# A four-layer graph network on one core: the last expert sums over edges before its own rows, and the closing scale and clip move

## The chip, the cores and the metric

The kernel runs on one core of one Trainium2 chip. The metric is the device time of one execution in microseconds (us), the median of several runs.

## The reference, cut to what matters

512 nodes with 512 features each pass through four graph layers; each layer sees `h = max(layernorm(x), 0)` and its result is added to `x`. The change lies in the end of the third layer and in the fourth.

```python
# layer 3: four experts of two convolutions each, the two best per node
def sage_conv(h, W_l, b_l, W_r):
    aggr = segment_sum(h[src], dst) * inv_deg
    return aggr @ W_l + b_l + h @ W_r
for e in range(4):
    h = x
    for l in range(2):
        h = relu(sage_conv(h, Wl[e, l], bl[e, l], Wr[e, l]))
out = sum over the top 2 experts of gate * h
# layer 4: graph convolution with self loops
H = X @ W + b
out = relu(segment_sum(H[src_f] * coef[:, None], dst_f))   # coef = isd[src] * isd[dst]
# and around each layer
h = max(layernorm(x), 0);  x = x + layer(h)
```

## The kernel before

Nodes are four row tiles of 128 (`NT = 4`), features four column tiles (`DT = 4`). The edges are held as a 512 x 512 matrix of counts, so each sum over edges is a matrix product. A float32 product is made of rounded parts: a matrix is split into `hi` and `lo`, and `mm3` (L1146 to L1148) multiplies hi by hi, hi by lo and lo by hi. The counts are exact, so a sum over edges (`sums_over_edges`, L1174 and L1175) takes two products for a tile, and a plain float32 product takes one instruction that the chip runs as two passes.

The order of all work is written out by hand, one instruction stream for each engine, with semaphores between them. PSUM (`ps`) has eight banks of 128 x 512 float32.

For each expert `e` TensorE makes, in this order: the hidden rows in banks 0 to 3; `z = hidden @ Wl` in banks 4 to 7; the expert's own rows `hidden @ Wr` in banks 0 to 3 (48 products); and the sum over edges of `z` in banks 4 to 7 (32 products). `z` is split by ScalarE (`z_hi`, L675) and VectorE (`z_lo`, L1069). VectorE adds the bias row `row_bl` to own rows (L1076, into `part`), ScalarE scales `part` by the node's gate (L682), VectorE adds the edge sums scaled by `inv_gate` (L1105), and clips and adds this to `x_sb` (L1110). `inv_gate` and `beats` are one buffer; it is made at L1078.

Behind the last expert comes the layer norm `LN5`. For each tile VectorE takes the statistics (L713 to L715), GpSimd a power (`rstd`, L471), VectorE the shift (L723), and ScalarE writes the normalised tile `h_sb` (L533). The last summation multiplies `h_sb` by `loop_hi`, the counts with self loops. The first `WHOLE` tiles go in as plain float32 (L1522), the others in two parts: `R_hi` by ScalarE (L690), `R_lo` by VectorE (L1118), products L1525 and L1526. The sum is split again (`agg_hi` L693, `agg_lo` L1122) and multiplied by the last weights; VectorE adds the bias row `b3_row` scaled by `reach` (L1135), ScalarE scales by `isd` and clips (L696), VectorE adds the mark of nodes without edges, `no_edge_nan`, and `x_sb` (L1130), and SyncE sends each tile out (L431). GpSimd makes the `lo` part of each weight matrix (L452, L453) and ScalarE the `hi` part (L528).

The order of the last expert's summation on TensorE is set by this piece:

```python
pe.wait_ge(z_lo_made, NT * (e + 1))
sums_over_edges(4, c_hi, c_lo, z_hi, z_lo, z_lo_made, NT * e, 1, near_done)
```

`together` (here 1) is the number of k tiles that are multiplied for all four goals before the rest is done goal by goal. Of VectorE's closing loops:

```python
norm_shift(LN5, NT - 1)
for t in range(WHOLE, NT):
    v.wait_ge(last_hi_made, t - WHOLE + 1)
    # R_lo[t] = h_sb[t] - R_hi[t]
```

Of the kernel before, what the change touches and what calls it, by code (L numbers as in the profile page):

```python
# [39 lines left out]
def build(nc, d, out):  # L40
# [193 lines left out]
    WHOLE = 2  # L234
# [10 lines left out]
    with ctx:  # L245
# [80 lines left out]
        last_done, last_sum, last_relu, x4_made = sem("last_done"), sem("last_sum"), sem("last_relu"), sem("x4_made")  # L326
# [197 lines left out]
        def _(act):  # L524
# [140 lines left out]
            for e in range(EXPERTS):  # L665
# [18 lines left out]
                if e < EXPERTS - 1:  # L684
                    split_hi(u + 5)
# [8 lines left out]
            for t in range(NT):  # L694
                act.wait_ge(last_sum, t + 1)
                nc.scalar.activation(tmp[:, t, :], tmp[:, t, :], ACT.Relu, scale=isd[:, t:t + 1])\  # L696
                  .then_inc(last_relu, 1)


        @block.vector  # L700
        def _(v):
# [291 lines left out]
            link(nc.vector.tensor_tensor(reach[:], reach[:], isd[:], ALU.add))  # L993

# [60 lines left out]

            for e in range(EXPERTS):
# [14 lines left out]
                v.wait_ge(bl_in[e % 2], 16 * (e // 2 + 1))  # L1071
# [29 lines left out]

                for t in range(NT):
                    v.wait_ge(near_done, NT * e + t + 1)
                    v.wait_ge(own_gated, NT * e + t + 1)
                    nc.vector.scalar_tensor_tensor(part[:, t, :], ps[:, 4 + t, :], inv_gate[:, t:t + 1],  # L1105
                                                   part[:, t, :], ALU.mult, ALU.add).then_inc(expert_sum, 1)
# [19 lines left out]
            b3_row = wait_row(B3)  # L1126

            def finish(t):
                v.wait_ge(last_relu, t + 1)
                nc.vector.scalar_tensor_tensor(x_sb[:, t, :], tmp[:, t, :], no_edge_nan[:, t:t + 1], x_sb[:, t, :],  # L1130
                                               ALU.add, ALU.add).then_inc(x4_made, 1)

            for t in range(NT):
                v.wait_ge(last_done, t + 1)
                nc.vector.scalar_tensor_tensor(tmp[:, t, :], b3_row[:], reach[:, t:t + 1], ps[:, 4 + t, :],  # L1135
                                               ALU.mult, ALU.add).then_inc(last_sum, 1)
                if t >= 1:
                    finish(t - 1)
            finish(NT - 1)


        @block.tensor
        def _(pe):
# [324 lines left out]
            for e in range(EXPERTS):  # L1468
# [25 lines left out]
                hi, lo = weights(FIRST_EXPERT + 4 * e + 3)  # L1494
                for t in range(NT):
                    for k in range(DT):
                        last = mm3(ps[:, t, :], hid_hi[:, k, col(t)], hid_lo[:, k, col(t)], hi[:, k, :],
                                   lo[:, k, :], k == 0, k == DT - 1)
                    last.then_inc(own_done, 1)

                pe.wait_ge(z_lo_made, NT * (e + 1))
                sums_over_edges(4, c_hi, c_lo, z_hi, z_lo, z_lo_made, NT * e, 1, near_done)


            pe.wait_ge(own_made, NT * EXPERTS)
# [62 lines left out]
```

## Time and profile before

| | us |
|---|---|
| median of 3 runs | 498.01 |
| the runs | 497.74, 500.13, 498.01 |
| the profiled execution's own time | 497.47 |
| its span | 495.7 |
| TensorE busy in the span | 458.0 (92%) |
| VectorE, ScalarE, GpSimd busy | 306.9, 192.0, 164.2 |

The span is what the profiler saw of one execution; the device time is 1.77 us longer. In the rows PE is TensorE, DVE VectorE, ACT ScalarE, POOL GpSimd, SP SyncE. Matmuls overlap in the array, so the distance between two starts says what one costs, not its length. The mean granted clock of TensorE over the span is 0.978 of full.

### The profile page before, as it was taken

The numbers are of one execution on the slowest core, as the hardware profiler recorded it, in microseconds if no ns is written. First come the engines' busy times: TensorE is split into PE (matmuls) and PEld (weight loads), VectorE is DVE, ScalarE is ACT, GpSimd is POOL, SyncE is SP. The second block draws the span as 40 slices with busy tenths as digits, with TensorE's granted clock in tenths as the row PEclk, the third lists the DMA queues.
The fourth block names the chain that finished last, engine by engine and source line by source line (L and its number), as shares of the span: only waits on it lengthen the run. The fifth ranks groups of instructions, "written<-read, shape, count | busy, mean of one in ns | idle before, by whom it ended". The sixth has DMA issues, their size and how long they took to land.

```text
span 495.7 us, 5939 instructions
## 1 busy us (share of the span) xinstructions
PE 458.0 (92%) x2107; PEld 334.1 (67%) x2107; DVE 306.9 (62%) x574; ACT 192.0 (39%) x264; POOL 164.2 (33%) x107
## 2 busy tenths in 40 slices
PE   4999996889869899899899999999999999999996
PEld 2465442334346778678678888888888888888654
DVE  5999836999975994877685333622362237133654
ACT  5888516546130631142441335123422252224232
POOL 3000131112243984448150433443344334343000
PEclk9999999899979999889998999999999999999999
DMA  8750000000030224203220032203420242120002
GB/s 265 202 225 1 1 1 22 0 1 0 1 106 0 72 100 170 85 1 117 77 86 0 19 127 110 86 2 109 161 87 3 91 141 89 41 85 1 0 1 85
DMA packets 22474, 34.34 MB, mean 69 GB/s; under 512 B 5680, under 2 KB 5936, under 8 KB 22448
## 3 DMA queue, kind: packets, MB, share of 16 engines
q1 hardware_dynamic: 22160, 33.85, 20.2%
q8 instruction: 18, 0.29, 0.2%
q10 hardware_dynamic: 288, 0.13, 0.1%
q14 instruction: 8, 0.07, 0.0%
HBM read 32.93 MB, written 1.05 MB: 69 GB/s over the span
## 4 chain that ended last, share of the span: by engine, by line
PE 63%; DVE 20%; issue 6%; POOL 5%; ACT 3%; DVEq 3%; DMA 1%; POOLq 0%
PE ps L1146 16%; PE ps L1148 16%; PE ps L1147 16%; PE ps L1208 4%; DVE one_src L784 3%; PE ps L1174 3%; PE ps L1175 3%; DVE rsum L886 2%; DVEq L784 2%; DVE e_sb L373 2%; DVE stats L713 2%; POOL x_sb L477 1%; PE ps L1287 1%; POOL w_lo L453 1%; PE ps L1159 1%
## 5 line engine op out<-in xcount | busy, mean ns | idle before, releaser
L452 POOL TENSOR_TENSOR w_lo<-w_stage,w_hi 128x1024 fp32r<-128x1024 f32 x22 | 52.7, 2395 | 137.7 <-ACT w_hi L528 137.7
L528 ACT ACTIVATE w_hi<-w_stage 128x2048 fp32r<-128x2048 f32 x23 | 43.9, 1910 | 73.1 <-PE ps L1148 73.1
L453 POOL TENSOR_TENSOR w_lo<-w_stage,w_hi 128x1024 fp32r<-128x1024 f32 x22 | 57.4, 2607 | 0.0
L1146 PE MATMUL ps<-w_hi,hid_hi 128*128 128x512 f32 x128 | 49.8, 389 | 0.0
L1147 PE MATMUL ps<-w_lo,hid_hi 128*128 128x512 f32 x128 | 49.8, 389 | 0.0
L1148 PE MATMUL ps<-w_hi,hid_lo 128*128 128x512 f32 x128 | 49.8, 389 | 0.0
L1063 DVE TENSOR_SCALAR tmp<-ps,bl 128x512 f32<-128x512 f32 x16 | 12.0, 751 | 52.2 <-ACT hid_hi L670 52.2
L1146 PE MATMUL ps<-T_hi,w_hi 128*128 128x512 f32 (+1 forms) x112 | 41.6, 372 | 1.8 <-DVE T_lo L743 1.4
L1148 PE MATMUL ps<-T_hi,w_lo 128*128 128x512 f32 (+1 forms) x112 | 40.7, 363 | 0.0
L1147 PE MATMUL ps<-T_lo,w_hi 128*128 128x512 f32 (+1 forms) x112 | 40.7, 363 | 0.0
L471 POOL TENSOR_TENSOR rstd<-vareps,scalars 128x1 f32<-128x1 f32 x24 | 15.8, 660 | 59.4 <-DVE vareps L715 59.4
L784 DVE TENSOR_SCALAR one_src<-iota_n,edge_m,edge_w 128x256 f16 x128 | 34.0, 332 | 0.0
L477 POOL TENSOR_TENSOR h_sb<-h_sb,row 128x512 f32<-128x512 f32 x8 | 11.1, 1403 | 55.8 <-DVE digits L798 48.7
L1076 DVE TENSOR_TENSOR part<-ps,row_bl 128x512 f32<-128x512 f32 x16 | 11.1, 691 | 29.9 <-PE ps L1148 29.9
L1069 DVE TENSOR_TENSOR z_lo<-ps,z_hi 128x512 fp32r<-128x512 f32 x16 | 10.9, 691 | 29.1 <-ACT z_hi L675 29.1
L1159 PE MATMUL ps<-ident,h_sb 128*128 128x128 f32 x64 | 13.5, 354 | 16.0 <-ACT h_sb L533 11.1
L608 ACT ACTIVATE s_bf<-ps 128x1024 bf16<-128x1024 f32 x16 | 16.4, 1023 | 30.4 <-PE ps L1287 22.3
L1147 PEld LDWEIGHTS ps<-w_lo,hid_hi 128*128 128x128 f32 x128 | 24.0, 188 | 5.0
L1146 PEld LDWEIGHTS ps<-w_hi,hid_hi 128*128 128x128 f32 x128 | 24.0, 188 | 5.0
L1148 PEld LDWEIGHTS ps<-w_hi,hid_lo 128*128 128x128 f32 x128 | 24.0, 188 | 5.0
L491 POOL TENSOR_TENSOR pool_sum<-e_sb 128x512 f32<-128x512 f32 x7 | 8.9, 1267 | 51.2 <-DVE rsum L884 31.6
L1146 PEld LDWEIGHTS ps<-T_hi,w_hi 128*128 128x128 f32 x112 | 21.6, 193 | 5.6 <-DVE T_lo L743 1.7
(206 smaller groups left out, 1064.4 us busy)
## 6 DMA issues: line engine op xcount, KB each, us to landing
w_stage<-in_L_gnn_Wr SPq DMA_DIRECT2D x8, 1024.0 KB, 5.3
w_stage<-in_L_gnn_Wl SPq DMA_DIRECT2D x8, 1024.0 KB, 5.2
w_stage<-in_L_gnn_W SPq DMA_DIRECT2D x5, 1024.0 KB, 6.3
x_sb<-in_x SPq DMA_DIRECT2D x4, 256.0 KB, 3.6
w_q<-in_L_gnn_Wq SPq DMA_DIRECT2D x1, 1024.0 KB, 7.8
w_k<-in_L_gnn_Wk SPq DMA_DIRECT2D x1, 1024.0 KB, 10.1
w_v<-in_L_gnn_Wv SPq DMA_DIRECT2D x1, 1024.0 KB, 5.7
w_o<-in_L_gnn_Wo SPq DMA_DIRECT2D x1, 1024.0 KB, 9.6
```

The lines of the kernel that those rows point to most:

```text
L452: gp.tensor_tensor(w_lo[s][:, 0:2], stage[s][:, 0:2], f32(w_hi[s][:, 0:2]), ALU.subtract)
L453: gp.tensor_tensor(w_lo[s][:, 2:4], stage[s][:, 2:4], f32(w_hi[s][:, 2:4]), ALU.subtract)\
L471: gp.tensor_tensor(rstd[:, n - 1:n], vareps[:, n - 1:n], half_neg, ALU.pow).then_inc(ln_rstd, 1)
L477: ins = gp.tensor_tensor(target[:, t, :], target[:, t, :], row[slot][:], ALU.add)
L528: nc.scalar.activation(w_hi[u % 2][:], stage[u % 2][:], ACT.Copy).then_inc(hi_made, 1)
L608: nc.scalar.activation(heads.rearrange("p (w b) n -> p w b n", w=2), group_scores(i, g), ACT.Copy)\
L784: last = nc.vector.tensor_scalar(one_src[:, bass.ds(slot, 1), :].squeeze(1), iota_n[:, 0:HALF], edge_m[:, 0, bass.ds(c, 1)], edge_w[:, bas ...
L1146: nc.tensor.matmul(goal, a_hi, b_hi, start=start, stop=False, **kw)
L1147: nc.tensor.matmul(goal, a_hi, b_lo, start=False, stop=False, **kw)
L1148: return nc.tensor.matmul(goal, a_lo, b_hi, start=False, stop=stop, **kw)
L1159: last = nc.tensor.transpose(ps[:, bank, col(j)], h_sb[:, t, col(j)], ident[:])
L1208: last = nc.tensor.matmul(ps[:, bank, :], src[:, k, col(t)], w[:, k, :], start=k == 0, stop=k == DT - 1)
```

## The change

1. In the last expert (`e == EXPERTS - 1`) TensorE sums over edges first, into banks 0 to 3 and with `together` 3, and makes own rows behind it, into banks 4 to 7.
2. ScalarE no longer scales own rows there; it writes `part = row_bl * gate` beforehand. VectorE adds the edge sums (`near_part`), then own rows scaled by the gate (`last_own`), which takes the place of L1105 in front of L1110. The additions of L1076 go for this expert.
3. `WHOLE` is 1: one plain tile in the last summation, three in two parts.
4. ScalarE writes the last bias row, scaled by `reach * isd`, into `tmp` before `LN5`; VectorE multiplies `reach` by `isd` once, in layer 2. VectorE adds `no_edge_nan` to `x_sb` beforehand (four instructions). At the end one VectorE instruction scales by `isd` and adds the bias, a second clips and adds to `x_sb`; ScalarE's clip L696 is gone.

```diff
-    WHOLE = 2
+    WHOLE = 1
...
@@ scalar
+                if e == EXPERTS - 1:
+                    act.wait_ge(bl_in[e % 2], 16 * (e // 2 + 1))
+                    for t in range(NT):
+                        act.wait_ge(x3_made, NT * e)
+                        nc.scalar.activation(part[:, t, :], row_bl[e % 2][:], ACT.Copy, scale=gate[:, t, e:e + 1])                          .then_inc(bl_gated, 1)
+                    break
...
+            act.wait_ge(reach_made, 1)
...
+            for t in range(NT):
+                nc.scalar.activation(tmp[:, t, :], row[b3_slot][:], ACT.Copy, scale=reach[:, t:t + 1])                  .then_inc(bias_row_made, 1)
...
-            for t in range(NT):
-                act.wait_ge(last_sum, t + 1)
-                nc.scalar.activation(tmp[:, t, :], tmp[:, t, :], ACT.Relu, scale=isd[:, t:t + 1])\
-                  .then_inc(last_relu, 1)
@@ vector
+            nc.vector.tensor_tensor(reach[:], reach[:], isd[:], ALU.mult).then_inc(reach_made, 1)
...
+            def near_part(e, t):
+
+                v.wait_ge(bl_gated, t + 1)
+                v.wait_ge(near_done, NT * e + t + 1)
+                nc.vector.scalar_tensor_tensor(part[:, t, :], ps[:, t, :], inv_gate[:, t:t + 1], part[:, t, :],
+                                               ALU.mult, ALU.add).then_inc(near_added, 1)
+
+            def last_own(e, t):
+
+                v.wait_ge(own_done, NT * e + t + 1)
+                v.wait_ge(near_added, t + 1)
+                nc.vector.scalar_tensor_tensor(part[:, t, :], ps[:, 4 + t, :], gate[:, t, e:e + 1], part[:, t, :],
+                                               ALU.mult, ALU.add).then_inc(expert_sum, 1)
...
-                for t in range(NT):
+                if e < EXPERTS - 1:
+                    v.wait_ge(bl_in[e % 2], 16 * (e // 2 + 1))
+                for t in range(NT if e < EXPERTS - 1 else 0):
...
+                if e == EXPERTS - 1:
+                    for t in range(NT):
+                        near_part(e, t)
...
-            b3_row = wait_row(B3)
+            for t in range(NT):
+                v.wait_ge(ln_out, ln_out_no(LN5, t))
+                nc.vector.tensor_scalar(x_sb[:, t, :], x_sb[:, t, :], no_edge_nan[:, t:t + 1], None, ALU.add)                  .then_inc(nan_added, 1)
 
             def finish(t):
-                v.wait_ge(last_relu, t + 1)
-                nc.vector.scalar_tensor_tensor(x_sb[:, t, :], tmp[:, t, :], no_edge_nan[:, t:t + 1], x_sb[:, t, :],
-                                               ALU.add, ALU.add).then_inc(x4_made, 1)
+                v.wait_ge(last_sum, t + 1)
+                v.wait_ge(nan_added, t + 1)
+                nc.vector.scalar_tensor_tensor(x_sb[:, t, :], tmp[:, t, :], 0.0, x_sb[:, t, :], ALU.max, ALU.add)                  .then_inc(x4_made, 1)
 
             for t in range(NT):
                 v.wait_ge(last_done, t + 1)
-                nc.vector.scalar_tensor_tensor(tmp[:, t, :], b3_row[:], reach[:, t:t + 1], ps[:, 4 + t, :],
+                v.wait_ge(bias_row_made, t + 1)
+                nc.vector.scalar_tensor_tensor(tmp[:, t, :], ps[:, 4 + t, :], isd[:, t:t + 1], tmp[:, t, :],
                                                ALU.mult, ALU.add).then_inc(last_sum, 1)
-                if t >= 1:
-                    finish(t - 1)
-            finish(NT - 1)
+                finish(t)
@@ tensor
+                if e < EXPERTS - 1:
+                    own_rows(0)
+                    pe.wait_ge(z_lo_made, NT * (e + 1))
+                    sums_over_edges(4, c_hi, c_lo, z_hi, z_lo, z_lo_made, NT * e, 1, near_done)
+                else:
+
+                    sums_over_edges(0, c_hi, c_lo, z_hi, z_lo, z_lo_made, NT * e, NT - 1, near_done)
+                    own_rows(4)
...
-            pe.wait_ge(own_made, NT * EXPERTS)
+            pe.wait_ge(near_added, NT)
```

TensorE's instructions where the last expert ends and the last summation begins, before. L1174 and L1175 are edge sums, L1522 the plain tiles, L1525 and L1526 the tiles in two parts; in brackets is what an instruction waits for.

```order
L1174 MATMUL ps<-z_hi,c_hi 128x512
L1175 MATMUL ps<-z_lo,c_hi 128x512
L1522 MATMUL ps<-loop_hi,h_sb 128x512 [waits ln_out,loop_made,own_made]
L1522 MATMUL ps<-loop_hi,h_sb 128x512 x3
L1522 MATMUL ps<-loop_hi,h_sb 128x512 [waits ln_out]
L1522 MATMUL ps<-loop_hi,h_sb 128x512 x3
L1525 MATMUL ps<-loop_hi,R_hi 128x512 [waits last_lo_made]
L1526 MATMUL ps<-loop_hi,R_lo 128x512
```

The same place in the changed kernel, where L1178 and L1179 are own rows, L1560 the plain tile, L1563 and L1564 the tiles in two parts:

```order
L1178 MATMUL ps<-w_lo_54,hid_hi 128x512
L1179 MATMUL ps<-w_hi_52,hid_lo 128x512
L1560 MATMUL ps<-loop_hi,h_sb 128x512 [waits ln_out,loop_made,near_added]
L1560 MATMUL ps<-loop_hi,h_sb 128x512 x3
L1563 MATMUL ps<-loop_hi,R_hi 128x512 [waits last_lo_made]
L1564 MATMUL ps<-loop_hi,R_lo 128x512
```

Own rows now stand directly ahead of the last summation, and the second tile waits for `R_lo` where it waited for `h_sb`.

VectorE's instructions from the last shift on, before:

```order
L723 SCALAR_TENSOR_TENSOR shift<-moments,rstd 128x1 [waits ln_rstd]
L1118 TENSOR_TENSOR R_lo<-h_sb,R_hi 128x512 [waits last_hi_made] x2
L1122 TENSOR_TENSOR agg_lo<-ps,agg_hi 128x512 [waits mix_hi_made] x4
L1135 SCALAR_TENSOR_TENSOR tmp<-row_110,node_cols,ps 128x512 [waits last_done,row_in0]
L1135 SCALAR_TENSOR_TENSOR tmp<-row_110,node_cols,ps 128x512 [waits last_done]
L1130 SCALAR_TENSOR_TENSOR x_sb<-tmp,node_cols,x_sb 128x512 [waits last_relu]
```

and in the changed kernel (`node_cols` holds `isd`, `reach` and `no_edge_nan`):

```order
L731 SCALAR_TENSOR_TENSOR shift<-moments,rstd 128x1 [waits ln_rstd]
L1148 TENSOR_TENSOR R_lo<-h_sb,R_hi 128x512 [waits last_hi_made] x3
L1152 TENSOR_TENSOR agg_lo<-ps,agg_hi 128x512 [waits mix_hi_made] x4
L1158 TENSOR_SCALAR x_sb<-x_sb,node_cols 128x512 [waits ln_out] x4
L1168 SCALAR_TENSOR_TENSOR tmp<-ps,node_cols,tmp 128x512 [waits bias_row_made,last_done]
L1163 SCALAR_TENSOR_TENSOR x_sb<-tmp,x_sb 128x512 [waits nan_added,last_sum]
```

There is a third `R_lo` behind the last shift, four additions stand between `agg_lo` and the closing pair, and the second of that pair waits for VectorE's own first.

## Rows read from the trace of the kernel before

**Rows 1.** The chain of waits, from the last expert's end: start us, us, what

```profile
461.01 2.47 issue
...
490.92 0.76 DVE tmp L1135
491.69 0.73 ACT tmp L696
492.45 0.75 DVE x_sb L1130
```

**Rows 2.** Timeline of PE: start us, us, engine line op out<-in, count, idle before

```profile
449.16 0.39 PE L1146 MATMUL ps<-w_hi,hid_hi 128*128 128x512 f32 x1
...
459.81 0.39 PE L1148 MATMUL ps<-w_hi,hid_lo 128*128 128x512 f32 x1
...
467.07 0.39 PE L1175 MATMUL ps<-z_lo,c_hi 128*128 128x512 f32 x1
467.97 7.11 PE L1522 MATMUL ps<-loop_hi,h_sb 128*128 128x512 f32 x16 [0.51 <-ACT h_sb L533]
475.49 0.50 PE L1525 MATMUL ps<-loop_hi,R_hi 128*128 128x512 f32 x1 [0.41 <-DVE R_lo L1118]
...
477.50 0.50 PE L1525 MATMUL ps<-loop_hi,R_hi 128*128 128x512 f32 x1
...
479.73 0.47 PE L1146 MATMUL ps<-w_hi,agg_hi 128*128 128x512 f32 x1
```

**Rows 3.** Timeline of DVE over the same stretch

```profile
447.95 2.73 DVE L1069 TENSOR_TENSOR z_lo<-ps,z_hi 128x512 fp32r<-128x512 f32 x4 [7.27 <-ACT z_hi L675]
...
460.24 0.69 DVE L1076 TENSOR_TENSOR part<-ps,row_bl 128x512 f32<-128x512 f32 x1 [2.03 <-PE ps L1148]
...
463.48 0.75 DVE L1105 SCALAR_TENSOR_TENSOR part<-ps,beats,part 128x512 f32<-128x512 f32 x1 [2.48 <-issue]
464.27 0.69 DVE L1110 SCALAR_TENSOR_TENSOR x_sb<-part,x_sb 128x512 f32<-128x512 f32 x1
...
466.07 0.74 DVE L1105 SCALAR_TENSOR_TENSOR part<-ps,beats,part 128x512 f32<-128x512 f32 x1
...
471.31 0.74 DVE L1105 SCALAR_TENSOR_TENSOR part<-ps,beats,part 128x512 f32<-128x512 f32 x1
...
474.67 0.16 DVE L723 SCALAR_TENSOR_TENSOR shift<-moments,rstd 128x1 f32<-128x1 f32 x1 [0.66 <-POOL rstd L471]
474.75 0.68 DVE L1118 TENSOR_TENSOR R_lo<-h_sb,R_hi 128x512 fp32r<-128x512 f32 x1
...
478.90 2.48 DVE L1122 TENSOR_TENSOR agg_lo<-ps,agg_hi 128x512 fp32r<-128x512 f32 x4 [1.83 <-ACT agg_hi L693]
```

**Rows 4.** L1105 over the whole span: ns min/median/max, first and last start

```profile
L1105 DVE SCALAR_TENSOR_TENSOR part<-ps,beats,part x16: 739/741/752, 311.1 to 471.3; 128x512 f32<-128x512 f32 x16
```

**Rows 5.** Timeline of ACT

```profile
449.85 1.91 ACT L528 ACTIVATE w_hi<-w_stage 128x2048 fp32r<-128x2048 f32 x1
...
460.97 0.72 ACT L682 ACTIVATE part<-part,gate 128x512 f32<-128x512 f32 x1 [2.00 <-DVE part L1076]
...
475.71 0.63 ACT L690 ACTIVATE R_hi<-h_sb 128x512 fp32r<-128x512 f32 x1
```

**Rows 6.** Timeline of POOL where the first L1105 ran

```profile
311.25 2.40 POOL L452 TENSOR_TENSOR w_lo<-w_stage,w_hi 128x1024 fp32r<-128x1024 f32 x1 [6.96 <-ACT w_hi L528]
```

**Rows 7.** The page, costliest groups: a VectorE operation with a scalar operand on 256 columns

```profile
L784 DVE TENSOR_SCALAR one_src<-iota_n,edge_m,edge_w 128x256 f16 x128 | 34.0, 332 | 0.0
```

**Rows 8.** Timeline of DVE in layer 2, where `reach` is made

```profile
231.08 2.32 DVE L993 TENSOR_TENSOR node_cols<-node_cols 128x4 f32<-128x4 f32 x1
...
236.72 0.69 DVE L998 TENSOR_TENSOR x_sb<-ps,x_sb 128x512 f32<-128x512 f32 x1 [1.40 <-PE ps L1148]
```

**Rows 9.** Two stretches: us, busy us (instructions) of each engine, granted clock, DMA

```profile
208.00:210.00 2.00, 1.09 (x4) 0.72 (x4) 1.89 (x6) 0.73 (x3) 0.55 (x1) 0.50 0.00 0
...
467.30:475.49 8.19, 7.27 (x18) 2.97 (x17) 7.14 (x18) 3.41 (x5) 1.65 (x3) 1.00 0.00 0
```

**Rows 10.** The chain of waits at the low clock, in layer 2

```profile
212.34 0.43 PE ps L1147
```

More of the change, by code:

```diff
@@ L325, in build @@
         mix_done, mix_hi_made, mix_lo_made = sem("mix_done"), sem("mix_hi_made"), sem("mix_lo_made")
-        last_done, last_sum, last_relu, x4_made = sem("last_done"), sem("last_sum"), sem("last_relu"), sem("x4_made")
+        last_done, last_sum, x4_made = sem("last_done"), sem("last_sum"), sem("x4_made")
+        bias_row_made, nan_added, reach_made = sem("bias_row_made"), sem("nan_added"), sem("reach_made")
+        bl_gated, near_added = sem("bl_gated"), sem("near_added")
         stored = sem("stored")
@@ L683, in _ @@
                       .then_inc(own_gated, 1)
-                if e < EXPERTS - 1:
-                    split_hi(u + 5)
+                split_hi(u + 5)
+            act.wait_ge(reach_made, 1)
+            b3_slot = rows_in[B3][1]
+            act.wait_ge(row_in[b3_slot], 16 * (1 + sum(s == b3_slot for _, s in rows_in[:B3])))
+            for t in range(NT):
+                nc.scalar.activation(tmp[:, t, :], row[b3_slot][:], ACT.Copy, scale=reach[:, t:t + 1])                  .then_inc(bias_row_made, 1)
             for t in range(NT):
@@ L1100, in _ @@
                         v.wait_ge(loop_lo_made, 3 * NT + 1)
+                if e == EXPERTS - 1:
+                    for t in range(NT):
+                        near_part(e, t)
                 for t in range(NT):
[L1103 to L1106, printed above, removed]
+                    if e == EXPERTS - 1:
+                        last_own(e, t)
+                    else:
+                        v.wait_ge(near_done, NT * e + t + 1)
+                        v.wait_ge(own_gated, NT * e + t + 1)
+                        nc.vector.scalar_tensor_tensor(part[:, t, :], ps[:, 4 + t, :], inv_gate[:, t:t + 1],
+                                                       part[:, t, :], ALU.mult, ALU.add).then_inc(expert_sum, 1)
                     if e == EXPERTS - 1 and t >= 1:
@@ L1493, in _, with own_rows @@
                             last.then_inc(z_done, 1)
[L1494 to L1502, printed above, removed]
-            pe.wait_ge(own_made, NT * EXPERTS)
+                def own_rows(bank):
+                    hi, lo = weights(FIRST_EXPERT + 4 * e + 3)
+                    for t in range(NT):
+                        for k in range(DT):
+                            last = mm3(ps[:, bank + t, :], hid_hi[:, k, col(t)], hid_lo[:, k, col(t)], hi[:, k, :],
+                                       lo[:, k, :], k == 0, k == DT - 1)
+                        last.then_inc(own_done, 1)
+                if e < EXPERTS - 1:
+                    own_rows(0)
+                    pe.wait_ge(z_lo_made, NT * (e + 1))
+                    sums_over_edges(4, c_hi, c_lo, z_hi, z_lo, z_lo_made, NT * e, 1, near_done)
+                else:
+                    sums_over_edges(0, c_hi, c_lo, z_hi, z_lo, z_lo_made, NT * e, NT - 1, near_done)
+                    own_rows(4)
+            pe.wait_ge(near_added, NT)
             pe.wait_ge(loop_made, NT)
```

1 line of the change is left out of this document (removed).

## The prediction, made before the changed kernel was run

> **What bounds the kernel now.** I read the chain of waits first. Up to 461.01 it is TensorE without a break, then a stretch that no engine holds alone, and the end is VectorE, ScalarE, VectorE on one tile [rows 1]. Then the timelines of TensorE and VectorE side by side from 449 us on. The reader should see three things in them.
>
> First, up to 467.07 TensorE issues a product each 0.227 us: 48 of own rows from 449.16 to 460.04 (10.88 us), 32 of edge sums behind them, 7.26 us [rows 2]. Then VectorE takes over. Its work for a tile (L1105, L1110, the statistics) repeats each 2.6 us, 463.48 to 466.07 [rows 3], but edge sums come out goal by goal, the first at about 463 and the last at 467.5, so three tiles queue up on VectorE. The fourth L1105 starts at 471.31, 3.8 us after TensorE had finished its bank. Second, from that start to the first product in two parts there are 4.18 us: 471.31 to 475.49, through `rstd`, the shift at 474.67 and `R_lo` at 474.75, which stands behind it [rows 2, 3]. Third, TensorE has little to do in that time: two plain tiles in 16 passes, 7.11 us, so about 0.43 from one to the next [rows 2]. The end of the program hangs on the fourth tile's layer norm, not on TensorE.
>
> **Edge sums first.** The swap leaves 80 products where there were 80, so TensorE is through at the same time if it never waits. The edge sums need `z_lo`; the first tile is ready at about 447.95 + 0.68 = 448.6, half a microsecond ahead of 449.16, and the fourth at 450.68, while k = 3 is first asked for after 24 products, at 454.6 [rows 3]. So no wait, and `together` 3 is what makes the third k tile wait for nothing. Own rows come out each 2.72 us (12 products), the last with the product at 467.07. VectorE started on an own row 0.43 us after its last product (459.81 to 460.24) [rows 2, 3], so the four `last_own` start at about 459.34, 462.06, 464.78 and 467.50. VectorE needs 2.6 us for a tile and gets one each 2.72: it keeps up, with 0.1 us to spare. The fourth starts at 467.50 in place of 471.31: **3.81 us** earlier on VectorE's side. `last_own` has L1105's form, 0.74 us [rows 4].
>
> What must be ready: the four `part = row_bl * gate` stand on ScalarE behind the weight copy that ends at 451.76, at most 0.72 each [rows 5], so they end by 454.6; the first edge sum needs 24 + 2 products, the last of them issued at 449.16 + 25 x 0.227 = 454.84, and VectorE sees it 0.43 us later, at about 455.3. Four `near_part` of at most 0.75 end by 458.3, one microsecond ahead of the first `last_own`. They run while GpSimd splits weights. So did the first L1105, at 311.1 with GpSimd's L452 from 311.25 on [rows 4, 6], and all 16 of them took 739 to 752 ns: none was held up. The four L1076 at 0.69 go; they were idle time's.
>
> **One plain tile.** Two plain tiles from 467.6 on would hold TensorE for 16 x 0.43 = 6.9 us, to about 474.5. One holds it to about 471.1. The second tile now needs `R_lo`, which stands behind the last shift: by the 4.18 us above it starts at 467.50 + 4.18 = 471.68. TensorE idles some 0.6 us there, then does three tiles. A tile took 475.49 to 477.50, 2.01 us with the start and the branch in it [rows 2]; a following one I put at 8 x 0.233 = 1.87. So the fourth tile starts at 471.68 + 2.01 + 1.87 = 475.56, against 477.50. `R_hi` of the fourth tile (before 475.71 to 476.34 [rows 5]) ends 3.8 us earlier, at 472.5, and its `R_lo` at 473.3: no wait. **Gain at the fourth tile 1.94 us.** From there to 479.73 and on to the last L1135 at 490.92 the work is the same, moved as a whole. So of the 3.81 us, 1.87 go to the third tile in two parts; with two plain tiles TensorE would be the bound and the gain about 0.9 us less.
>
> **The closing pair.** Before, L1135, ScalarE's L696 and L1130 start at 490.92, 491.69 and 492.45 and end at 493.20, 2.28 us [rows 1]. Now two instructions of VectorE follow each other as L1105 and L1110 do: 463.48 to 464.27 is 0.79, and the second has L1110's form, 0.69 [rows 3]; 1.48 us. **Gain 0.80 us.** By the cycle table of the Trainium skill (VectorE: DVE Perf Modes, the section on the TRN2 errata, 58 cycles plus one for each element from SBUF to SBUF) an estimate of the second instruction is 0.59 us and the gain would be 0.1 us larger; the row has 0.69, and I go by the row.
>
> **The rest, at nothing.** The four additions of `no_edge_nan` have no counterpart in the trace. Bounds: 0.33 us (scalar form on half as many columns [rows 7]) and 0.75 (an operation that reads PSUM too [rows 4]); I take 0.69, that of a full SBUF tile. They start when `agg_lo` ends, 481.38 - 1.94 = 479.44 [rows 3], and end by 482.4 at the upper bound; the first tile's closing pair begins three tiles of 2.04 us (9 products) before the fourth's, at 490.92 - 1.94 - 6.12 = 482.9. After that the pair's 1.48 us fit between tiles. The four scaled bias rows of ScalarE run from 454.6 to 457.5, the first normalisation starts at about 463. The product `reach * isd` in layer 2 follows an instruction that took 2.32 us on four columns; 1.40 us later VectorE idles for TensorE [rows 8]. I take 0.15 us, at most 2.3, of which 1.4 are covered: 0, at most 0.9. Output copies: one each 2.04 us, the last as long as before.
>
> **The sum** is 1.94 + 0.80 = 2.74 us. The profiled execution (497.47, span 495.7) becomes 494.7 (span 493.0). It lies 0.54 below the median of the runs shown; from that median, 498.01 - 2.74 = **495.3 us**, 0.55% less. About 0.5%, 2.5 us, is what a measurement of this kernel can tell from no change, so the forecast is just past it.
>
> **Rivals.**
>
> *VectorE falls behind by tiles.* The margin is 0.1 us for each of three tiles. If a tile costs 2.9 us in place of 2.6 (two semaphores to wait for where it was one), the fourth `last_own` starts at 459.34 + 3 x 2.9 = 468.04, 0.5 us late; if `near_part` also ends 1 us behind its cover, 1.5 us late. The time is 495.8 to 496.8, no change by the bound. For it: the margin is small. Against it: four tiles before ran at 2.6 in each case. Chance 0.22, with the reach product's 0.9 us in it.
>
> *More than forecast.* The span ends 2.5 us behind the last L1130 (493.20 to 495.7), and the third tile's copy was issued only 0.9 us ahead of the fourth's; now they are 2.04 us apart. If 0.4 us of the 2.5 were that, and the later tiles of the summation start 0.2 us quicker than I put them, the time is 494.7. Chance 0.1.
>
> *The change of order is hidden*: TensorE waits at 449.16 for `z_lo` and everything behind moves by what the sum gains. That takes `z_lo` late by 3 us where the trace has it 0.5 us early. Time 498. Chance 0.04.
>
> *Slower: the clock.* At 208 to 210 TensorE was busy 1.09 of 2 us and its granted clock stood at 0.50, the lower of its two levels, 1.2 GHz [rows 9]; products then came each 0.43 us [rows 10], not 0.227. The change puts a new idle piece at 471.1 to 471.7, ahead of 24 + 48 = 72 products on the path. At the low level each costs 0.2 us more: all of them 14.6 us, a time of 509.9. It decides from 26 of the 72 on (2.74 + 2.5 us over 0.2). Against it: in the stretch of 8.19 us that has both idle pieces of before, 0.51 and 0.41, the clock was 1.00 throughout [rows 2, 9], and the new order has half the plain passes and one idle piece, with own rows issued densely ahead of it. The Trainium skill (TensorE: Matmul & The Clock Gate, on the clock gate) says that the throttled state is the default and that only activity lifts it; by that rule a thinner stretch here is what could bring it down. Chance 0.04.
>
> *The change does not do what it says.* The orders above show it on both engines; what could fail is only that the waits bind elsewhere, which is the first rival.
>
> **How the numbers follow.** Forecast 0.6, VectorE behind 0.22, more 0.1, hidden 0.04, clock 0.04. The predicted time is the forecast's, 495.3. The range: down to 494.3, which is the 494.7 of the case with more and 0.4 us for the spread of the runs (two of the three are 0.27 apart); up to 496.8, the end of the first rival; the two unlikely ones are left out. Faster by over 0.5% means below 495.5: most of the forecast's 0.6 (0.53 of it, as it passes the bound by only 0.25 us), and the 0.1 of the case with more: 0.63. Within 0.5%: the rest of the forecast, the first rival and the hidden case, 0.33. Slower: the clock, 0.04.
>
> **What would show it.** In the profile after: edge sums of the last expert from 449.2 without a gap; the fourth `last_own` near 467.5; one plain tile of eight passes; the first product in two parts near 471.7 and the fourth tile's near 475.6; the four `no_edge_nan` additions over before the first closing pair; closing pair of 1.5 us with no ScalarE in it; clock 1.00 to the end. It is wrong if VectorE's `last_own` starts later than 0.5 us after its own row's last product, if `R_lo` of the fourth tile is what its products wait for, or if the closing instructions queue.

## The result, and the profile after the change

The changed kernel takes **494.5 us** (median of 7 runs, 493.78 to 496.18), the kernel before 498.01 (497.56 to 500.13 in the 7 runs beside it). The ratio is 0.9923, with a 95% interval of 0.9903 to 0.9943: 0.8% less, where 0.55% was forecast. By the ratio that is 3.8 us, a time of 494.2; by the medians it is 3.5; the forecast was 2.74. The sign was right, the gain larger.

The profiled execution took 493.78 us (span 491.9, before 495.7). The summary of the profile's page hides nearly all of the change: TensorE has the same 2107 products and the same share of the span.

```profile
span 491.9 us, 5957 instructions
...
PE 454.6 (92%) x2107; PEld 333.7 (68%) x2107; DVE 309.4 (63%) x580; ACT 192.4 (39%) x265; POOL 164.3 (33%) x107
```

So I went to the end of the chain of waits, as before [rows 1] (start us, us, what):

```profile
467.30 2.13 issue
...
470.20 0.61 DVE R_lo L1148
470.86 0.50 PE ps L1563
...
475.31 0.61 ACT agg_hi L706
475.95 0.70 DVE agg_lo L1152
476.79 0.47 PE ps L1177
...
487.97 0.76 DVE tmp L1168
488.75 0.69 DVE x_sb L1163
```

No ScalarE stands in the closing part any more. The chain passes from the layer norm to TensorE at 470.86, which is the second tile, and from there on TensorE does not wait until `agg_hi`. Before, the chain's last release came later, at the third tile. The timeline of TensorE shows the places that the forecast named (start us, us, engine line op out<-in, count, idle before and what ended it):

```profile
448.38 0.39 PE L1205 MATMUL ps<-z_hi,c_hi 128*128 128x512 f32 x1
...
466.28 0.39 PE L1179 MATMUL ps<-w_hi,hid_lo 128*128 128x512 f32 x1
466.51 3.59 PE L1560 MATMUL ps<-loop_hi,h_sb 128*128 128x512 f32 x8
470.86 0.50 PE L1563 MATMUL ps<-loop_hi,R_hi 128*128 128x512 f32 x1 [0.76 <-DVE R_lo L1148]
...
474.66 0.39 PE L1563 MATMUL ps<-loop_hi,R_hi 128*128 128x512 f32 x1
```

All 80 products of the last expert follow each other without a gap. One plain tile takes eight passes, then TensorE idles 0.76 us (forecast some 0.6), then come three tiles in two parts. The fourth, at 474.66, has a first product of 0.39 us and no idle time ahead; before it began with one of 0.50 [rows 2], the form that the first product behind a wait has.

VectorE over the same stretch:

```profile
454.58 2.73 DVE L1069 SCALAR_TENSOR_TENSOR part<-ps,beats,part 128x512 f32<-128x512 f32 x4 [4.61 <-PE ps L1206]
458.55 0.75 DVE L1076 SCALAR_TENSOR_TENSOR part<-ps,gate,part 128x512 f32<-128x512 f32 x1 [1.25 <-PE ps L1179]
...
461.27 0.75 DVE L1076 SCALAR_TENSOR_TENSOR part<-ps,gate,part 128x512 f32<-128x512 f32 x1
...
466.71 0.75 DVE L1076 SCALAR_TENSOR_TENSOR part<-ps,gate,part 128x512 f32<-128x512 f32 x1
...
470.05 0.16 DVE L731 SCALAR_TENSOR_TENSOR shift<-moments,rstd 128x1 f32<-128x1 f32 x1 [0.66 <-POOL rstd L473]
470.12 1.29 DVE L1148 TENSOR_TENSOR R_lo<-h_sb,R_hi 128x512 fp32r<-128x512 f32 x2
471.75 0.69 DVE L1148 TENSOR_TENSOR R_lo<-h_sb,R_hi 128x512 fp32r<-128x512 f32 x1 [0.35 <-ACT R_hi L703]
475.95 2.48 DVE L1152 TENSOR_TENSOR agg_lo<-ps,agg_hi 128x512 fp32r<-128x512 f32 x4 [3.50 <-ACT agg_hi L706]
478.35 1.67 DVE L1158 TENSOR_SCALAR x_sb<-x_sb,node_cols 128x512 f32<-128x512 f32 x4
481.85 0.75 DVE L1168 SCALAR_TENSOR_TENSOR tmp<-ps,node_cols,tmp 128x512 f32<-128x512 f32 x1 [1.84 <-PE ps L1179]
...
487.97 0.75 DVE L1168 SCALAR_TENSOR_TENSOR tmp<-ps,node_cols,tmp 128x512 f32<-128x512 f32 x1 [0.56 <-PE ps L1179]
488.75 0.69 DVE L1163 SCALAR_TENSOR_TENSOR x_sb<-tmp,x_sb 128x512 f32<-128x512 f32 x1
```

The four `last_own` (L1076) start 2.72 us apart, as own rows come out. The second tile's `R_lo` stands behind the shift at 470.05, which waits for `rstd`; the same two instructions ended TensorE's idle piece before [rows 3]. The additions of `no_edge_nan` (L1158) are over at 480.02, 1.84 us ahead of the first closing pair. The clock was at its higher level from 467 to 476 (stretch in us, length, busy us and instructions of PE, PEld, DVE, ACT, POOL, granted clock, DMA share, GB/s):

```profile
467.00:476.00 9.00, 8.24 (x30) 5.32 (x29) 4.39 (x11) 3.58 (x6) 0.84 (x2) 1.00 0.01 2
```

**Measured from the last expert's start.** Executions differ ahead of the change too, so absolute starts mislead: the 80 products begin at 449.16 before and at 448.38 after. I call the time from there to the end of the span the tail, and measure in it:

| us from the first of the 80 products to | before | after | earlier by | forecast |
|---|---|---|---|---|
| second tile in two parts (before: third) | 26.33 | 22.48 | 3.85 | 3.81 |
| fourth tile | 28.34 | 26.28 | 2.06 | 1.94 |
| first product with the last weights | 30.57 | 28.41 | 2.16 | 1.94 |
| last closing pair | 41.76 | 39.59 | 2.17 | 1.94 |
| end of VectorE | 44.04 | 41.06 | 2.98 | 2.74 |
| end of the span (the tail) | 46.5 | 43.5 | 3.0 | 2.74 |

Of a gain of 3.5 to 3.8 us, 3.0 lie in the tail and 0.5 to 0.8 ahead of it, where the diff has only one small instruction, the product `reach * isd` in layer 2. The experiments had two tasks: to put a price on each part in the tail, and to find what shifts the part ahead of it.

### The profile page after: what moved, and what is told of

Same layout as the page of the kernel before. It is cut to its first block, busy times and chain, and to the rows that moved or that the text cites. A ratio compares the mean times of both kernels' runs of the same rounds, so it can differ in the third digit from the quotient of the medians.

```text
span 491.9 us, 5957 instructions
## 1 busy us (share of the span) xinstructions
PE 454.6 (92%) x2107; PEld 333.7 (68%) x2107; DVE 309.4 (63%) x580; ACT 192.4 (39%) x265; POOL 164.3 (33%) x107
## 4 chain that ended last, share of the span: by engine, by line
PE 70%; DVE 17%; POOL 5%; issue 3%; ACT 3%; DMA 1%; SPq 0%; POOLq 0%; DVEq 0%
PE ps L1177 15%; PE ps L1179 15%; PE ps L1178 15%; PE ps L1246 6%; PE ps L1239 4%; PE ps L1206 3%; PE ps L1205 3%; DVE rsum L894 3%; PE ps L1232 3%; DVE e_sb L375 2%; DVE stats L721 2%; POOL x_sb L479 1%; POOL w_lo L455 1%; DMA x_sb<-in_x 1%; DVE half_sum L891 1%
## 5 line engine op out<-in xcount | busy, mean ns | idle before, releaser
L1178 PE MATMUL ps<-w_lo,hid_hi 128*128 128x512 f32 x128 | 49.8, 389 | 0.0
L1179 PE MATMUL ps<-w_hi,hid_lo 128*128 128x512 f32 x128 | 49.8, 389 | 0.0
L1178 PE MATMUL ps<-T_lo,w_hi 128*128 128x512 f32 (+1 forms) x112 | 40.7, 364 | 0.0
L1179 PE MATMUL ps<-T_hi,w_lo 128*128 128x512 f32 (+1 forms) x112 | 40.7, 363 | 0.0
L792 DVE TENSOR_SCALAR one_src<-iota_n,edge_m,edge_w 128x256 f16 x128 | 35.1, 399 | 0.0
L1179 PEld LDWEIGHTS ps<-w_hi,hid_lo 128*128 128x128 f32 x128 | 24.0, 188 | 5.0
L1178 PEld LDWEIGHTS ps<-w_lo,hid_hi 128*128 128x128 f32 x128 | 24.0, 188 | 5.0
L1177 PE MATMUL ps<-agg_hi,w_hi 128*128 128x512 f32 x64 | 24.9, 389 | 0.0
```

The costliest lines, as they stand in the source:

```text
L792: last = nc.vector.tensor_scalar(one_src[:, bass.ds(slot, 1), :].squeeze(1), iota_n[:, 0:HALF], edge_m[:, 0, bass.ds(c, 1)], edge_w[:, bas ...
L1177: nc.tensor.matmul(goal, a_hi, b_hi, start=start, stop=False, **kw)
L1178: nc.tensor.matmul(goal, a_hi, b_lo, start=False, stop=False, **kw)
L1179: return nc.tensor.matmul(goal, a_lo, b_hi, start=False, stop=stop, **kw)
```

## The experiments

The theory: the whole gain lies in the tail, 2.2 us of it through the order and the plain tile and 0.8 through the closing pair. Its rivals: the closing pair's gain is covered by the output copies; the cut from two plain tiles to one brings the gain by itself, without the order; the rest of the gain is a second effect of the change ahead of the tail, or else a difference between executions. Each expectation says in its own words what the theories it names would give. Ratios are to runs of the kernel before on the same chip.

**Both kernels again** (no edit; five more runs of the change, twelve of before).

> The kernel before, unchanged, run beside itself. I measure two things in its profile: the stretch ahead of the last expert's first product behind z (449.16 us in the profile shown, 448.38 in the changed kernel's) and the stretch from there to the span's end, the tail (46.54 and 43.52). Theory A (the change acts in the tail alone, 3.0 us; the 0.8 us ahead of it are a difference from one execution to the next that any two profiles of the same kernel can have): the tail is 46.5 within 0.1, the stretch ahead of it anything from 448 to 450, the ratio 1.000 within its interval. Rival B (the change also shortens the stretch ahead of the tail by 0.8 us, through another order of work or code): this kernel shows 449.2 ahead of its tail, the changed ones 448.4.

> The changed kernel again. Theory A: tail 43.5 within 0.1, the stretch ahead of it from 448 to 450, so the ratio between 0.992 and 0.996. Rival B: 448.4 ahead of the tail and a ratio of 0.992 again.

Before: ratio 1.0005 (0.9990 to 1.0020), tail 46.6. After: 494.08 us, 0.9917 (0.9902 to 0.9933), tail 43.5. Both tails repeat to 0.1 us, and the larger gain comes again (0.9917, a little beyond the 0.992 to 0.996 that the theory allowed). But the profiled execution of the change had a span of 494.1, 2.2 longer than the first, and all of it lay ahead: the 80 products began at 450.59 in place of 448.38.

**Two plain tiles** (the change with `WHOLE` back at 2).

```diff
-    WHOLE = 1
+    WHOLE = 2
```

> The changed kernel with two plain tiles in the last summation. Theory A: TensorE goes from own rows into 16 plain passes without a wait, 16 x 0.43 = 6.9 us, so the third tile starts 7.0 us behind own rows and the fourth at 44.0 - 17.1 from the end; the tail is 44.1, 0.6 longer than with one plain tile, still 2.4 shorter than before. Rival C (the number of plain tiles plays no part, since the fourth tile's layer norm sets the start of its products): tail 43.5, no idle of TensorE gone.

The tail was 44.0, half a microsecond more than with one. TensorE, not VectorE, then sets when tiles in two parts begin:

```profile
470.51 7.03 PE L1560 MATMUL ps<-loop_hi,h_sb 128*128 128x512 f32 x16
476.97 0.79 PE L1563 MATMUL ps<-loop_hi,R_hi 128*128 128x512 f32 x1
```

There is no idle entry at the second row. In whole times, 494.38 (0.9926, 0.9907 to 0.9944), half a microsecond cannot be seen.

**The closing pair alone** (before, with the bias rows on ScalarE, the `reach * isd` product, the early additions and the new closing instructions; the order of the last expert and `WHOLE` 2 as before).

```diff
+            act.wait_ge(reach_made, 1)
...
+            for t in range(NT):
+                nc.scalar.activation(tmp[:, t, :], row[b3_slot][:], ACT.Copy, scale=reach[:, t:t + 1])
...
-            for t in range(NT):
-                act.wait_ge(last_sum, t + 1)
-                nc.scalar.activation(tmp[:, t, :], tmp[:, t, :], ACT.Relu, scale=isd[:, t:t + 1])
```

> The kernel before with the closing pair, the bias row and the no-edge additions of the change, but own rows first and two plain tiles. Theory A: the tail is 46.54 - 0.81 = 45.7. Rival D (the closing pair gains more than its own 0.8 us, since the last two output copies stand apart): below 45.4, with the piece behind the last VectorE instruction under 2.3 us where it was 2.5.

The tail was 45.7, 0.8 less, and the time from the last VectorE instruction to the end of the span 2.47 us, 2.50 before: the output copies cover nothing of it. VectorE's last pair:

```profile
490.16 0.75 DVE L1142 SCALAR_TENSOR_TENSOR tmp<-ps,node_cols,tmp 128x512 f32<-128x512 f32 x1 [0.56 <-PE ps L1153]
490.94 0.69 DVE L1137 SCALAR_TENSOR_TENSOR x_sb<-tmp,x_sb 128x512 f32<-128x512 f32 x1
```

490.16 to 491.63 is 1.47 us, where three instructions took 2.28 [rows 1]. Ratio 0.9979 (0.9954 to 1.0005).

**The order and the one plain tile, without the closing pair** (the change with the closing part of before: the edit above, reversed).

> The changed kernel with the closing instructions of before (edge sums first and one plain tile stay). Theory A: tail 43.52 + 0.81 = 44.3, a ratio of 0.9955. Rival: the parts are not additive, and the tail differs from 44.3 by more than 0.2.

Tail 44.25, 2.3 less than before's; ratio 0.9965 (0.9947 to 0.9983). With the 0.8 of the closing pair the parts add up to 3.1: they are independent, and the tail is explained. The run with two plain tiles splits the 2.2: its tail of 44.0, with the closing pair's 0.8 taken out, leaves 1.7 us for the order, and the plain tile adds 0.5.

**One plain tile without the new order** (before with `WHOLE` at 1).

```diff
-    WHOLE = 2
+    WHOLE = 1
```

> The kernel before with one plain tile only, own rows still first. Theory A (two plain tiles were right for the old order): three tiles in two parts stand behind the last shift at 474.7, so the fourth starts 1.8 us later than before; tail 48.3 to 48.4, ratio 1.004. Rival C (the count of plain tiles plays no part): 46.5.

**Slower**: 502.11 us, 1.0069 (1.0048 to 1.0089), tail 49.6. I expected 48.3 to 48.4 and missed by 1.3 us. The timeline of TensorE and three stretches suggest why:

```profile
470.29 3.67 PE L1522 MATMUL ps<-loop_hi,h_sb 128*128 128x512 f32 x8 [0.52 <-ACT h_sb L533]
477.81 0.80 PE L1525 MATMUL ps<-loop_hi,R_hi 128*128 128x512 f32 x1 [3.85 <-DVE R_lo L1118]
...
480.11 0.63 PE L1526 MATMUL ps<-loop_hi,R_lo 128*128 128x512 f32 x1
480.54 0.58 PE L1525 MATMUL ps<-loop_hi,R_hi 128*128 128x512 f32 x1
480.96 0.39 PE L1526 MATMUL ps<-loop_hi,R_lo 128*128 128x512 f32 x1
```

```profile
473.00:477.00 4.00, 0.96 (x3) 0.13 (x1) 3.16 (x10) 1.88 (x3) 1.10 (x2) 1.00 0.00 0
477.00:481.00 4.00, 3.19 (x8) 2.54 (x9) 2.05 (x4) 1.44 (x2) 0.00 (x0) 0.57 0.01 4
481.00:485.00 4.00, 4.00 (x18) 2.96 (x16) 0.69 (x2) 1.32 (x3) 0.00 (x0) 1.00 0.00 0
```

With edge sums last, the second tile's layer norm ends as late as ever, and one plain tile less leaves TensorE idle for 3.85 us. Behind that the granted clock fell near the lower level (0.57, that is mostly 1.2 GHz) for 3 us of products, each 0.43 us after the last in place of 0.23. This is my slower rival's mechanism; whether the clock is the whole of the 1.3 us the next run tests. The Trainium skill (TensorE: Matmul & The Clock Gate, on the clock gate) says that idleness brings the throttled state back; the trace agrees here, behind 3.85 us, and has 1.00 behind the change's idle piece of 0.76 us.

**The same with TensorE kept busy** (the kernel above, and 16 products into an unused bank in the idle time; nothing reads them).

```diff
+                    if k == 1:
+                        pe.wait_ge(expert_sum, NT * (EXPERTS - 1) + 1)
+                        for _ in range(16):
+                            nc.tensor.matmul(ps[:, 4, :], R_hi[:, 0, col(0)], loop_hi[:, 0, :], start=True, stop=True)
```

> The kernel before with one plain tile, and 16 products into bank 4, whose results nobody reads, between the plain tile and the second (3.6 us in a wait of 3.85 us). Its forerunner without them had a tail of 49.63 where the order of work gives 48.35: TensorE idled 3.85 us, then the granted clock stood at half and eight products took 0.43 us each. Theory F (the missing 1.3 us are the clock, and idle time brought it down): clock 1.00 through the tail, tail 48.35 to 48.5. Rival G (the 1.3 us are something else in the order of three tiles in two parts): tail 49.6 again.

Tail 48.2 (expected 48.35 to 48.5), 1.4 less, at a clock of 1.00; time 500.21, ratio 1.0036 (1.0010 to 1.0061).

```profile
470.72 4.23 PE L1514 MATMUL ps<-loop_hi,R_hi 128*128 128x512 f32 x16
475.14 0.50 PE L1529 MATMUL ps<-loop_hi,R_hi 128*128 128x512 f32 x1 [0.19 <-DVE R_lo L1118]
...
474.00:478.00 4.00, 3.81 (x18) 2.82 (x17) 2.06 (x4) 1.44 (x2) 0.29 (x1) 1.00 0.02 4
```

That settles the 1.3 us as the clock's: the plain tile's work did more than fill a wait, it held the clock. It also refutes the rival that the plain tile's removal gains by itself: without the new order it costs 1.7 us even at full clock.

**`R_lo` ahead of the last shift.** In the change the second tile's `R_lo` waits behind a shift that itself waits for GpSimd. Moved ahead of it:

```diff
-            norm_shift(LN5, NT - 1)
-            for t in range(WHOLE, NT):
...
+            last_lo(1)
+            norm_shift(LN5, NT - 1)
+            last_lo(2)
+            last_lo(3)
```

> The changed kernel with the second tile's R_lo ahead of the last shift on VectorE, in the 0.66 us in which VectorE waits for the power. Theory A (the 0.76 us of TensorE's idle time ahead of the second tile are this instruction's place in the queue): the second tile starts 0.7 us earlier, the tail is 42.8, a ratio of 0.991. Rival E (the fourth tile's R_lo is bound by the same chain): tail 43.5, with the idle time now ahead of the fourth tile.

The tail fell to 42.7, from 43.5. TensorE has no idle piece left:

```profile
470.47 3.59 PE L1565 MATMUL ps<-loop_hi,h_sb 128*128 128x512 f32 x8
473.99 0.50 PE L1568 MATMUL ps<-loop_hi,R_hi 128*128 128x512 f32 x1
```

But its median was 496.19 us (0.9935, 0.9903 to 0.9967), above the change's, with runs from 492.44 to 497.37. The profiled execution began the 80 products at 452.34. On this chip the kernel before had 498.27, so whole times show 2.1 us where the tails show 3.9: something ahead of the tail moves by more than this edit is worth.

**`R_lo` earlier still** (the second tile's between the fourth `last_own` and its addition to `x_sb`, the third's ahead of the shift).

> The same, with the second tile's R_lo still earlier (between the fourth last_own and its addition to x_sb) and the third's ahead of the last shift. The layer norm of the fourth tile is then 0.7 us later, its R_lo about 1.4 us later than in the changed kernel, where it stood ready 2.2 us ahead of its products. Theory A: TensorE never idles, the tail is 42.6 to 42.7. Rival E: the delay of the fourth tile reaches TensorE, tail 43 or more.

Tail 42.7 again; time 493.56, 0.9914 (0.9887 to 0.9941). The addition to `x_sb` now comes later, and the fourth tile waits for its own `R_lo`:

```profile
474.49 0.50 PE L1569 MATMUL ps<-loop_hi,R_hi 128*128 128x512 f32 x1
```

What starts earlier on one side is given back on the other; the simpler version above is as good.

**Both kernels a third time**, twelve runs each.

> The kernel before a third time, beside the changed one on one chip. Theory A: tail 46.55. The stretch ahead of it has varied from 448.4 to 452.4 between profiles of all kernels, with how long the clock stays low behind the gate logits (264 us); if the change has no part in that, the two kernels' runs differ by the tail's 3.0 us, plus or minus what that variation leaves in the median (0.5 us).

> The changed kernel a third time. Theory A: tail 43.52, a ratio to the kernel before of 0.994 (3.0 us), within 0.001. Rival B (the change also wins 0.5 to 1 us in the stretch ahead of the tail, as the first two ratios of 0.9923 and 0.9917 would have it): 0.992 a third time, with the median 3.8 us or more below.

Before 499.09 (1.0009, 0.9987 to 1.0031), after 494.09 (0.9925, 0.9904 to 0.9946). Tails 46.6 and 43.5. The theory had 0.993 to 0.995 for the ratio, the rival with a gain ahead of the tail 0.992 and 3.8 us or more between the medians: the ratio lies between the two, and the medians, 5.0 apart, speak for the rival. The profiled execution of the change took 498.44, nearly 5 us more than its first (493.78), and all of that lay ahead of the tail: 453.03 against 448.38. The granted clock tells where. In layer 2, at 257 us, 48 products of four columns (the gate logits) follow each other each 0.11 us. In ten of the 13 profiles with this code the clock was 1.00 from 256 to 260; in three it was lower already there, 0.94, 0.94 and, with one plain tile in the old order, 0.88:

```profile
256.00:260.00 4.00, 4.00 (x33) 3.92 (x32) 2.61 (x5) 1.26 (x2) 0.00 (x0) 0.88 0.54 205
```

The three stretches from 260 on, first of before:

```profile
260.00:264.00 4.00, 4.00 (x27) 3.75 (x27) 2.61 (x5) 1.26 (x2) 0.00 (x0) 0.79 0.00 0
264.00:268.00 4.00, 4.00 (x15) 3.18 (x14) 3.17 (x19) 0.22 (x1) 0.00 (x0) 0.78 0.00 0
268.00:272.00 4.00, 4.00 (x19) 3.30 (x19) 1.62 (x10) 0.00 (x0) 0.00 (x0) 1.00 0.00 0
```

then of the change's first execution:

```profile
260.00:264.00 4.00, 4.00 (x22) 3.61 (x22) 2.54 (x7) 1.26 (x2) 0.00 (x0) 0.70 0.00 0
264.00:268.00 4.00, 4.00 (x17) 3.19 (x16) 3.10 (x19) 0.22 (x1) 0.00 (x0) 0.87 0.00 0
268.00:272.00 4.00, 4.00 (x19) 3.33 (x18) 1.01 (x6) 0.00 (x0) 0.00 (x0) 1.00 0.00 0
```

and of its third, the 498.44:

```profile
260.00:264.00 4.00, 4.00 (x21) 4.00 (x22) 2.58 (x4) 1.28 (x3) 0.00 (x0) 0.53 0.02 4
264.00:268.00 4.00, 4.00 (x14) 3.54 (x15) 2.24 (x10) 0.46 (x2) 0.00 (x0) 0.50 0.00 0
268.00:272.00 4.00, 4.00 (x14) 3.19 (x13) 3.00 (x18) 0.00 (x0) 0.00 (x0) 0.70 0.00 0
```

TensorE is busy for the whole 12 us in each, and still the clock falls, for a time that differs between executions of one and the same kernel. The missing clock, (1 - clock) x 4 us summed over the three rows, is 1.7 us in the first two and 5.1 in the last, 3.4 more. Of the 4.65 us by which the last one's tail began later, 3.3 lie between the first logit product and the tail. The other 1.4 were there before the logits: they began at 256.44 in the first execution, at 257.82 in the third.

Put together for all 13 profiles, the time from the first logit product to the start of the tail takes only three values, whichever kernel it is:

| from logits to tail, us | profiles of kernels with the old order | with the new order |
|---|---|---|
| 191.9 to 192.0 | before (2), closing pair alone, one plain tile with filling | the change (1) |
| 193.6 | before (1) | the change (1), the change without the closing pair, `R_lo` earlier still |
| 195.2 | one plain tile | the change (1), two plain tiles, `R_lo` ahead of the shift |

and the start of the logits lies anywhere from 255.5 to 257.8 us. The sums of missing clock, from 256 to 272, are 1.7, 3.4 and 5.1 us for the three. In the four profiles with 195.2 the clock fell in the middle of the logits, 2 to 3 us after the first of them, in the other nine 4 to 5.5 us after it, toward their end. The length (3.3 us between the ends) and the start (2.3 us) make the executions of one kernel differ; both orders of the last expert have all three lengths.

**The same three kernels with the clock kept high in that stretch.** After every third gate-logit product one product of 512 columns is put into bank 0, which the expert's hidden rows overwrite later (the logits are in bank 3): 16 in all, unread.

```diff
+                    nc.tensor.matmul(ps[:, 0, :], T_hi[:, k, col(t)], T_hi[:, k, :], start=True, stop=True)
```

> The kernel before with 16 products of 512 columns between the 48 four-column products of the gate logits, into bank 0, results unread: 3.6 us more work. Three times before, the granted clock fell to half there and stayed so for 3.4 to 9 us. Theory H (the spread ahead of the tail, 448 to 453 us, is that stretch): clock 1.00 through it, the loss of 1.7 to 4.5 us goes, so the median moves by between -1 and +2 us, and the runs lie within 1.5 us of each other in place of 4. Rival: the clock falls all the same, the median is 3.6 us higher and the spread the same.

> The changed kernel with the same 16 products. Theory H with A: the difference between the medians of this and of the kernel before with the same products is the tail's 3.0 us (2.7 to 3.3), since what the changed kernel had beyond that (0.9 us) came from how often its runs met a short stretch of low clock. Rival B (it has a true gain ahead of the tail): 3.6 us or more.

> The kernel with the second tile's R_lo ahead of the last shift, with the same 16 products. Theory A: 0.86 us below the changed kernel with them, as its tail is shorter by that; 3.9 below the kernel before with them.

The clock stays at 1.00 from 256 to 272 in all three profiles, and from the logits to the tail all three kernels take 194.0 us. Of before:

```profile
260.00:264.00 4.00, 4.00 (x31) 3.71 (x29) 2.46 (x4) 1.26 (x2) 0.00 (x0) 1.00 0.00 0
264.00:268.00 4.00, 4.00 (x24) 3.44 (x23) 1.90 (x12) 0.22 (x1) 0.00 (x0) 1.00 0.00 0
```

| with the 16 products | runs | median (range), us | ratio (95%) | tail |
|---|---|---|---|---|
| before | 12 | 499.02 (498.25 to 501.02) | 1.0016 (0.9997 to 1.0036) | 46.5 |
| the change | 8 | 496.16 (495.1 to 497.5) | 0.9946 (0.9925 to 0.9968) | 43.5 |
| `R_lo` ahead of the shift | 6 | 494.9 (494.21 to 495.82) | 0.9921 (0.9895 to 0.9947) | 42.7 |

The change against before is now 2.86 us by the medians, and the tails' difference is 3.0: the surplus over the tail is gone, as far as intervals of 1 us each way can say. `R_lo` ahead of the shift brings 1.26 more by the medians where its tail says 0.8 (the two intervals overlap); whole times had hidden its advantage before. The spread shrank to 2.8, 2.4 and 1.6 us, where the kernel before had 496.66 to 501.25 in its 19 runs on the same chip and the change 493.41 to 498.44 in its last 12; I had expected it within 1.5, and fewer runs make part of the smaller spreads of the last two. What is left is the start of the logits, 256.57, 258.09 and 257.00 in the three profiles. Stretches of low clock stand ahead of it too, near 88, 144 and 208 us, and most of them also miss about 1.7 or 3.4 us of clock; nothing was done about these, and what they do to the start was not measured. The 16 products cost more than they give back in the median: before +0.6 us beside its own runs, the change +2 beside its earlier ones. They are a tool of measurement, not an improvement.

## Why the prediction was right and wrong

**The step that failed is the sum, "1.94 + 0.80 = 2.74 us": it has no term for anything ahead of the last expert's 80 products, and its tile term is too small.** By the ratio the gain is 3.8 us, 1.1 more than the sum. The tail has 3.0 of it; with that alone the time would be 495.0, inside the range. The other 0.8 stand ahead, where the prediction had put the product in layer 2 "at most 0.9" on the side of a loss. The time by the ratio, 498.01 x 0.9923 = 494.2, lies just under the range's lower end, 494.3; the median, 494.5, lies just inside, so the range was missed by little and would with other luck have held. In the two parts:

- The tile term, 1.94, measured 2.17. The start of the second tile in two parts was right to 0.04 us. I put the two tiles behind it at 2.01 + 1.87 = 3.88 us; they took 3.80. And I moved the work behind the fourth tile "as a whole", though the fourth tile had itself started behind a wait before (2.23 us from its first product to the first one with the last weights) and no longer does (2.13).
- Ahead of the tail the sum has nothing, and the runs showed 0.5 us (by the medians) to 0.8 (by the ratio). Executions differ there by up to 5 us, most of it through the stretch of low clock in layer 2. I had looked for low clock only where the change is. Three shown runs with two 0.27 apart are no measure of a spread, and one row of the windows at 260 to 268, 0.79 and 0.78, would have told that a stretch with a busy TensorE is not at full clock there. With the clock kept high there in both kernels, the difference is 2.9 us, near the 2.74.

What remains open: why the change gains more than its tail explains, in three separate sets of runs (3.8, 4.1 and 3.7 us by the ratios 0.9923, 0.9917 and 0.9925, against 3.0). That it goes with the low stretch is likely, since with the clock kept high there it is gone (2.86 against a tail of 3.0); the intervals there, 0.002 of 499 or 1 us each way, don't prove it. The change's runs would have to meet the shortest of the three lengths more often than those of before, and whole times of runs without a profile don't tell a length from a late start of the logits. Their mean granted clocks over the whole span say more. The one instruction that the change adds ahead of the stretch is the product in layer 2, 0.16 us at 233.02. Of the kernels that have it, 16 of 55 runs show a mean clock of 0.984 or more (3 of 12 with the closing pair alone); of those without it, none of 139 does (113 of before, 12 of the change without the closing pair, 14 with one plain tile in the old order). The only profile of such a run, the change's first at 0.985, has the shortest length and few low stretches ahead of it. With the 16 products put in, both kinds have such runs, 5 of 12 before and 7 of 14 with the change. So the surplus is probably an effect of the change on the low stretch, and not chance. That this product makes it is not shown, since no run has it alone, and the cause stays open. Why an execution gets one length or another was not found either.

**Point by point.**
- *Edge sums first*: no wait for `z_lo`, the 80 products without a gap, as said; the fourth `last_own` 18.33 us into the tail, forecast 18.34 (467.50 - 449.16). `near_part` ran from 454.58 to 457.31, 1.24 us ahead of the first `last_own`. Right.
- *VectorE keeps up with 0.1 us to spare*: right; it needed 2.67 to 2.68 us of each 2.72 (458.55 to 461.22), so 0.05. The first rival (0.22) did not happen.
- *One plain tile*: right, with 0.76 us idle for 0.6. "With two plain tiles ... about 0.9 us less": measured 0.5.
- *The closing pair*: 0.80 forecast, 0.81 measured, and shown alone. The second instruction took 0.69 us, as the row of before had it; the 0.59 that I had worked out from the Trainium skill (VectorE: DVE Perf Modes, the errata's cycle table) was too low; the page itself says that this row gives too little for a single operation.
- *The rest, at nothing*: right for what it names in the tail; what it left out ahead of the tail is above. The additions of `no_edge_nan` took 1.67 us for four, 0.42 each and not 0.69; the reach product 0.16.
- *More than forecast* (0.1, 494.7): in its time (494.7) this is the case that came nearest, but by luck for the larger part: later tiles were quicker by 0.2 us, as it says, but the 2.5 us behind the last instruction stayed (2.46), in the closing-pair run too, and the rest lay ahead of the tail.
- *The clock* (0.04): not here, 1.00 from 467 to 476. The mechanism is real and cost 1.4 us where the idle piece was 3.85 us long. My price, 72 products at the low level, was far too high: only the first seven products came at the low level, then the clock was back at 1.00.

## What to carry to other kernels

Before judging an edit of a few microseconds, compare two executions of the same kernel by stage: if they differ ahead of the edit by as much as the edit is worth, measure from the last common point to the end, or hold the varying stretch steady in both kernels. When an edit lets a tile start earlier, ask at each later step whether it still starts behind a wait: here the first product behind one cost 0.1 us more, and that was half of the 0.23 that the term missed. Work that only fills TensorE's idle time can't simply be dropped: without the reorder that made its successor ready, it cost 3 us, 1.4 of them through the clock.

## What the runs showed of the hardware

- The granted clock fell to 0.50 toward the end of 48 products of four columns (nine profiles of 13) or in the middle of them (four), though TensorE was busy without a break, and what it cost came in three sizes, 1.7, 3.4 and 5.1 us of missing clock, in different executions of one kernel. With a 512-column product after every third it stayed at 1.00, in three profiles of three.
- An idle piece of 3.85 us was followed by some 3 us of products at half rate; one of 0.76 us was not.
- A scalar addition on VectorE from SBUF to SBUF, 128 x 512 in float32, takes 0.42 us. An operation on two tensors takes 0.69, with both in SBUF (L1163) and with one in PSUM (L1076 of before, 690 to 692 ns in all 16). With a column of scalars beside them it takes 0.75, from PSUM (L1168) and from SBUF alone (L1130 of before, 743 to 751 ns). So the extra 0.06 goes with the column, not with PSUM as the prediction's bound had it. The Trainium skill (VectorE: DVE Perf Modes, the table of performance tiers) puts the float32 scalar form in the doubled tier, which the 0.42 bears out; I had taken it at 0.69.
